# Layer 1 of a four-layer kernel: f and g projected by image row into four bands of 32 partitions, bias and "plus one" on ScalarE, one tanh per row group

## The reference, cut to what matters

```python
def _L1_conv_ref(x, Wf, bf, Wg, bg, Wh, bh):      # Wf, Wg: 256 x 32, Wh: 256 x 256
    f = jnp.einsum('bhwc,ck->bhwk', x, Wf) + bf
    g = jnp.einsum('bhwc,ck->bhwk', x, Wg) + bg
    h = jnp.einsum('bhwc,co->bhwo', x, Wh) + bh
    scores = jnp.einsum('bhik,bhjk->bhij', f, g)   # 64 x 64 for each image row
    attn = jax.nn.sigmoid(scores)
    out = jnp.einsum('bhij,bhjo->bhio', attn, h)
    return out
def _L2_conv_ref(...):                             # the end of it
    gate = jax.nn.sigmoid(feats).reshape(b, h, w, 1)
    return gate * x
x = x + _L1_conv_ref(_gn(x), ...)
```

## Time and profile before

| what | value |
|---|---|
| median of three runs | 5786.15 us (5784.26 to 5790.85) |
| profiled execution | 5781.0 us, its span 5779.1 us |
| PE busy | 5346.3 us, 93% of the span |
| DVE busy | 4160.8 us, 72% |
| ACT busy | 4086.9 us, 71% |
| POOL busy | 1926.3 us, 33% |
| mean granted TensorE clock | 0.952 of full |

### The profile page before, as it was taken

The page is one execution under the profiler, slowest core; times in us unless marked ns, Lnnn a source line. Parts: engine busy times, 40 slices in busy tenths (PEclk is TensorE's granted clock), DMA queues, the critical chain, the costliest instruction groups (busy, mean ns, idle before and its releaser), DMA issues.

```text
span 5779.1 us, 111762 instructions
## 1 busy us (share of the span) xinstructions
PE 5346.3 (93%) x43240; PEld 2801.0 (48%) x43240; DVE 4160.8 (72%) x8715; ACT 4086.9 (71%) x6385; POOL 1926.3 (33%) x1588
## 2 busy tenths in 40 slices
PE   7799999989999999999999999999999999999886
PEld 3435445363553645446364453645446354453624
DVE  8467777777777777677777777777677777777726
ACT  1467768677786867768677785777868678686794
POOL 2224243342423424233341423424233242433402
PEclk9799999999999999999999999999999999999996
DMA  2010201102011020101102011020101102011000
GB/s 80 8 38 12 65 25 47 39 5 72 17 60 30 14 64 12 64 26 34 50 7 69 21 59 30 12 64 14 61 28 31 50 10 67 22 52 36 3 30 30
DMA packets 163165, 211.10 MB, mean 37 GB/s; under 512 B 13136, under 2 KB 146000, under 8 KB 162640
## 3 DMA queue, kind: packets, MB, share of 16 engines
q1 hardware_dynamic: 138064, 136.82, 7.3%
q0 software_dynamic: 24576, 67.14, 4.0%
HBM read 136.80 MB, written 67.11 MB: 35 GB/s over the span
## 4 chain that ended last, share of the span: by engine, by line
PE 70%; ACT 13%; DVE 9%; issue 5%; POOL 2%; DMA 1%; ACTq 0%; DVEq 0%; POOLq 0%; SPq 0%
PE PS L1190 34%; PE PS L1365 15%; PE PS L1356 6%; PE PS L1460 2%; ACT n_x L505 2%; PE PS L1224 2%; PE PS L1248 2%; PE PS L1299 2%; ACT big L579 1%; DVE stats L843 1%; ACT work L543 1%; ACT work L542 1%; ACT soft L579 1%; ACT xin L505 1%; ACT attn L551 1%
## 5 line engine op out<-in xcount | busy, mean ns | idle before, releaser
L579 ACT ACTIVATE big<-PS 128x1024 f32<-128x1024 f32 x1376 | 1365.3, 1024 | 458.9 <-PE PS L1356 397.2
L579 ACT ACTIVATE soft<-PS 128x1024 f32<-128x1024 f32 x672 | 676.0, 1024 | 359.3 <-PE PS L1356 349.9
L400 POOL DMA_INDIRECT quant_H<-emb_t,idx x512 | 487.4, 952 | 981.8 <-DVE idx L867 790.0
L1190 PE MATMUL PS<-e_hi,n_hi 128*128 128x512 f16 x2048 | 781.7, 382 | 20.2 <-DVE m L861 10.7
L1190 PE MATMUL PS<-e_lo,n_hi 128*128 128x512 f16 x2048 | 778.3, 380 | 0.0
L1190 PE MATMUL PS<-e_hi,n_lo 128*128 128x512 f16 x2048 | 778.1, 380 | 0.0
L1365 PE MATMUL PS<-big,w 128*4 128x512 f32 x5504 | 759.8, 641 | 0.0
L843 DVE BATCH_NORM_STATS2 stats<-XT 128x6 f32<-128x512 f32 x1024 | 651.7, 683 | 12.4 <-POOL XT L416 2.5
L867 DVE FIND_INDEX8 idx<-m,work 128x8 uint32<-128x1024 f32 x512 | 622.2, 1219 | 0.0
L1356 PE MATMUL PS<-rhs,lhs 12*128 12x512 bf16 x4096 | 563.9, 398 | 59.6 <-ACT big L579 37.3
L861 DVE CUSTOM_DVE_ANT_0 work<-PS,e_bias,m 128x512 f32<-128x512 f32 x512 | 384.1, 750 | 213.1 <-PE PS L1190 207.1
(11 more groups left out here) (216 smaller groups left out, 11134.1 us busy)
## 6 DMA issues: line engine op xcount, KB each, us to landing
xin<-x SPq DMA_DIRECT2D x128, 512.0 KB, 3.8
out<-yout SPq DMA_DIRECT2D x128, 512.0 KB, 2.9
quant_H<-emb_t,idx POOLq DMA_INDIRECT x512, 2.7
XT<-emb SPq DMA_DIRECT2D x1, 1024.0 KB, 6.0
XT<-wh SPq DMA_DIRECT2D x1, 256.0 KB, 5.9
XT<-wqv SPq DMA_DIRECT2D x1, 256.0 KB, 6.2
XT<-wk SPq DMA_DIRECT2D x1, 128.0 KB, 6.1
w_sb<-w SPq DMA_DIRECT2D x1, 128.0 KB, 5.9
```

Source lines behind the costliest of these rows:

```text
L400: nc.gpsimd.indirect_dma_start(quant[:, g % 2, u, :], None, emb_t, bass.IndirectOffsetOnAxis(ap=idx[:, t % (2 * GT), 0:1], axis=0),).then_ ...
L579: nc.scalar.activation(E[h % 3][:, z * 1024:(z + 1) * 1024], bank(2 * z, 2), ACT.Exp).then_inc(exped.sem, 1)
L1190: ins = mm(dst, a, b, start=first and j == 0, stop=last and j == 2)
```

## The change

Four things change; the lists of steps are the same.

1. `l1_fg` on PE goes by image row. f and g of even rows (r = 0) and odd rows (r = 1) go to four bands of 32 partitions in bank 4: f of r = 0, f of r = 1, g of r = 0, g of r = 1. Each band takes six products of 32 rows by 256 columns, whose moving operand picks four runs of 64 pixels with a stride of 128. That is 24 matmuls for a group. The bias product goes away, with onesel, its memsets and the setup that splits the bias.
2. ACT moves f (64 x 256) and g (64 x 256) with one instruction each, and adds the bias in it from a column of 64 floats. FT and GTm lie on partitions 0 to 63, r = 1 on 32 to 63; `l1_scores` reads them there. The bias comes by four DMAs of 32 floats in place of one of 96 x 64.
3. The tanh is one instruction of 128 x 256 into a new place (tanhs, part of work); the two that add 1 read it there and write the diagonal blocks.
4. Of the gate, ACT adds 1 itself, behind its exponential, and DVE only takes the reciprocal.

```diff
-        FT = work[0:CK, 0:1024].rearrange("p (s w n) -> p s w n", s=2, w=2)
-        GTm = work[0:CK, 1024:2048].rearrange("p (s w n) -> p s w n", s=2, w=2)
+        FT = work[0:2 * CK, 0:512].rearrange("p (s n) -> p s n", s=2)
+        GTm = work[0:2 * CK, 512:1024].rearrange("p (s n) -> p s n", s=2)
+        tanhs = work[:, 1024:1536].rearrange("p (s n) -> p s n", s=2)
...
-                (bfg_f, bfg.partition_broadcast(96)),
                 (bo_f, b_out.partition_broadcast(P)),
+                *((fg_bias[(2 * j + w) * CK:(2 * j + w + 1) * CK, :], bfg[j * CK:(j + 1) * CK].unsqueeze(1))
+                  for j in range(2) for w in range(2)),
...
             def l1_fg(im, g):
                 act.wait_ge(*l1_scored.room(im, g, 2))
                 act.wait_ge(*l1_fged.after(im, g))
-                for w in range(2):
-                    r = 2 * CK * w
-                    nc.scalar.activation(FT[:, g % 2, w, :], PS[r:r + CK, 4, 0:2 * P], copy)
-                    last = nc.scalar.activation(GTm[:, g % 2, w, :], PS[r + CK:r + 2 * CK, 4, 0:2 * P], copy)
+                if im + g == 0:
+                    act.wait_ge(weights_in, 16 * NW)
+                for j, kept in enumerate((FT, GTm)):
+                    rr = slice(2 * CK * j, 2 * CK * (j + 1))
+                    last = nc.scalar.activation(kept[:, g % 2, :], PS[rr, 4, 0:2 * P], copy, bias=fg_bias[rr, 0:1])
                 last.then_inc(l1_fgkept.sem, 1)
...
-                for r in range(2):
-                    rr = slice(r * ROW, (r + 1) * ROW)
-                    last = nc.scalar.activation(attn[rr, g % 2, :, rr],
-                                                PS[rr, 4, 0:GT * ROW].rearrange("p (u i) -> p u i", u=GT), ACT.Tanh, scale=0.5)
-                last.then_inc(l1_tanhed.sem, 1)
+                nc.scalar.activation(tanhs[:, g % 2, :], PS[:, 4, 0:GT * ROW], ACT.Tanh, scale=0.5).then_inc(l1_tanhed.sem, 1)
                 act.wait_ge(*l1_tanhed.after(im, g))
                 for r in range(2):
                     rr = slice(r * ROW, (r + 1) * ROW)
-                    last = nc.scalar.activation(attn[rr, g % 2, :, rr], attn[rr, g % 2, :, rr], copy, bias=ones[rr, 0:1])
+                    last = nc.scalar.activation(attn[rr, g % 2, :, rr], tanhs[rr, g % 2, :].rearrange("p (u i) -> p u i", u=GT),
+                                                copy, bias=ones[rr, 0:1])
...
             def gate_exp(im):
                 act.wait_ge(*gate_arg.after(im))
                 nc.scalar.activation(gate[:, 1, :], gate[:, 0, :], ACT.Exp, scale=-1.0).then_inc(gate_exped.sem, 1)
+                act.wait_ge(*gate_exped.after(im))
+                nc.scalar.activation(gate[:, 1, :], gate[:, 1, :], copy, bias=ones[:, 0:1]).then_inc(gate_oned.sem, 1)
...
-                dve.wait_ge(*gate_exped.after(im))
-                link(v.tensor_scalar(gate[:, 1, :], gate[:, 1, :], 1.0, None, ALU.add))
+                dve.wait_ge(*gate_oned.after(im))
                 v.reciprocal(gate[:, 2, :], gate[:, 1, :]).then_inc(gate_made.sem, 1)
...
-                products = [(fg_bias, None)]
+                products = []
                 for k in range(KC):
                     products += [(fg_hi[:, k, :], n_hi[:, g % 2, k, :]), (fg_hi[:, k, :], n_lo[:, g % 2, k, :]),
                                  (fg_lo[:, k, :], n_hi[:, g % 2, k, :])]
                 for j, (weight, part) in enumerate(products):
-                    for w in range(2):
-                        moving = onesel[:, 0:2 * P] if part is None else part[:, w * 2 * P:(w + 1) * 2 * P]
-                        ins = mm(PS[64 * w:64 * w + 64, 4, 0:2 * P], weight[:, 0:2 * CK], moving,
-                                 start=j == 0, stop=j == len(products) - 1)
+                    for f in range(2):
+                        for r in range(2):
+                            rr = slice((2 * f + r) * CK, (2 * f + r + 1) * CK)
+                            ins = mm(PS[rr, 4, 0:GT * ROW], weight[:, f * CK:(f + 1) * CK],
+                                     part.rearrange("p (u r i) -> p r u i", u=GT, r=2)[:, r, :, :],
+                                     start=j == 0, stop=j == len(products) - 1, skip_group_check=True)
...
                 for u in range(GT):
                     for r in range(2):
-                        cols = slice(u % 2 * P + r * ROW, u % 2 * P + (r + 1) * ROW)
-                        ins = mm(PS[r * ROW:(r + 1) * ROW, 4, u * ROW:(u + 1) * ROW], GTm[:, g % 2, u // 2, cols],
-                                 FT[:, g % 2, u // 2, cols], start=True, stop=True)
+                        cc, cols = slice(r * CK, (r + 1) * CK), slice(u * ROW, (u + 1) * ROW)
+                        ins = mm(PS[r * ROW:(r + 1) * ROW, 4, cols], GTm[cc, g % 2, cols], FT[cc, g % 2, cols],
+                                 start=True, stop=True)
```

More of the change, by code:

```diff
@@ L110, in build @@
         ones = sb("ones", [P, P])
-        onesel = sb("onesel", [96, 2 * P], BF16)
         mhalf = sb("mhalf", [P, GT])
@@ L117, in build @@
         fg_lo = sb("fg_lo", [P, KC, 2 * CK], F16)
-        fg_bias = sb("fg_bias", [96, 2 * CK], BF16)
+        fg_bias = sb("fg_bias", [P, 1])
         h_hi = sb("h_hi", [P, KC, C], F16)
@@ L250, in build @@
         filled, exped, summed = step("filled", 2 * HALVES), step("exped", 2 * HALVES, 2), step("summed", HALVES, 3)
-        acc_kept, acc_turned, gate_arg, gate_exped, gate_made = (
-            step(n, 1) for n in ("acc_kept", "acc_turned", "gate_arg", "gate_exped", "gate_made"))
+        acc_kept, acc_turned, gate_arg, gate_exped, gate_oned, gate_made = (
+            step(n, 1) for n in ("acc_kept", "acc_turned", "gate_arg", "gate_exped", "gate_oned", "gate_made"))
         g_normed, g_spread = step("g_normed"), step("g_spread")
@@ L298, in build @@
         wfg_f = xt_w[:, 5376:5504].rearrange("p (k n) -> p k n", k=KC)
-        rows_r = xt_w[0:96, 5504:5568]
-        bfg_f = xt_w[0:96, 5568:5632]
         bo_f = xt_w[:, 5632:5888]
@@ L303, in build @@
         wmean = xt_w[:, 6144:6148]
-        NW = 12
+        NW = 15
         @block.sync
@@ L763, in link @@
                 dve_chain.link(dve, ins)
-            for t, val in ((ones, 1.0), (mhalf, -0.5), (attn, 0.0), (w2, 0.0), (ctxd, 0.0), (onesel, 0.0), (m8, BIG)):
+            for t, val in ((ones, 1.0), (mhalf, -0.5), (attn, 0.0), (w2, 0.0), (ctxd, 0.0), (m8, BIG)):
                 setup_link(v.memset(t[:], val))
             setup_link(v.memset(bank(4), 0.0))
-            for j in range(3):
-                setup_link(v.memset(onesel[32 * j:32 * j + 1, :], 1.0))
             for f in range(2):
@@ L798, in prepare @@
                 if part == 3:
-                    for j in range(3):
-                        rr = slice(32 * j, 32 * j + 32)
-                        setup_link(v.tensor_copy(fg_bias[rr, :], bfg_f[rr, :]))
-                        for q in range(j + 1, 3):
-                            tail = slice(32 * q, 32 * q + 32)
-                            setup_link(v.tensor_copy(rows_r[tail, :], fg_bias[rr, :]))
-                            setup_link(v.tensor_tensor(bfg_f[tail, :], bfg_f[tail, :], rows_r[tail, :], ALU.subtract))
                     setup_link(v.tensor_reduce(wmean[:, 0:1], wo_f, AX, ALU.add))
```

## The result

The changed kernel takes 5632.5 us (median of 4 runs, 5627.4 to 5634.2) where the kernel before takes 5785.2 beside it (4 runs, 5780.0 to 5790.9): 0.9734 of the time, 95% interval 0.9718 to 0.9751. The forecast was 5671 us, with a range from 5636. The direction held; the gain was 153 us where 115 were forecast, and the time fell 3.5 us under the range's lower end.

The account below looks back on a forecast made before the run. PE, 93% busy, bounds it, alternating with ACT in layer 1's stretches. Fifteen stretches x 7.3 = 110 us, with 3 from the first stretch and 2.5 setup, 115 less: 5666, plus 5 to the median, 5671 us; range 5636 to 5738.

Parts of the forecast that it names:

- Copies: ACT's copies of f and g: two at 0.468 us replace four of 0.375, 0.56 us less a group.
- Tanh: ACT's tanh in layer 1: one of 128 x 256 replaces two of 0.378 us, 0.38 us less a group.
- The gate's add on ScalarE: Gate's plus one, 2.151 us on DVE, takes 0.30 on ACT: chain 1.85 us shorter in fifteen images.
- The reciprocal at its own length: DVE's reciprocal behind the gate's add is not stalled by POOL; if it were, all 1.85 us would stay.
- Projections: PE's f and g products: seven pairs become six fours at 0.11 us each, 0.9 us less a stretch.
- Scores: Layer 1's eight fp32 score products on PE stay at 0.68 us a group.
- The idle: PE's idle in a layer 1 stretch: half of today's 8.1 us stays, 4.0 us, giving 59.9 us a stretch.
- The clock: Lower clock costs PE some 3.8 us in thirteen of fifteen layer 1 stretches; 2.6 come back, 2.3 us a stretch.
- lower end: Fastest bound: 2 us of PE idle a stretch, 9.3 us less each, 147 less in all, 5639 us.
- Rival 1: PE's idle in layer 1 stretches stays as DVE and PE wait for each other: 52 us less, 5734; chance 0.16.
- Rivals 2, 3 and 4: Fours two by two, about 5755 us (0.05); scores one by one, 5730 (0.07); fours one by one, 5890 (0.05).
- Rival 4's turning point: Change turns slower where a group's projections cost over 0.77 + 0.8 us, a four above 0.26 us.

Follow-up runs that it names:

- e5: Changed kernel with each copy of f and g cut in two (32 partitions each): 5735.4 us.
- e6: Changed kernel with the tanh cut in two instructions of 64 x 256: 5683.4 us.
- e7: Changed kernel with one spare product of all four bands in each group's projections: 5639.7 us.
- e2: Kernel before with only the gate's plus one moved to ScalarE: 5739.1 us.
- e3: Changed kernel with the gate's plus one back on DVE: 5692.4 us.
- e12: e3 with fifteen idle-filling products on PE ahead of its wait for the gate: 5675.2 us.
- e1: Kernel before with fifteen idle-filling products on PE ahead of the gate's wait and fifteen ahead of the third group's scores: 5737.5 us.
- e10: Changed kernel with five idle-filling products ahead of each of the first waits for an exponential in the distances: 5626.2 us.
- e9: Kernel before with the edits of e1 and e2 together: 5736.0 us.
- e11: Changed kernel with the lower 64 partitions of the tanh's plus one moved to DVE as a tensor-tensor add: 5785.1 us.
- e4: Changed kernel with attn as two 64-row halves, output products in two row groups, one plus-one instruction, DVE's sum in four instructions: 5761.0 us.

## Why the prediction fell short

Step by step, as the prediction put them:

- Copies, forecast 0.468 us: 0.465. Tanh 0.38: 0.383. The gate's add on ScalarE 0.30: 0.321. The reciprocal at its own length: 0.353. All right. On the chain the prediction took the copies of six groups and the tanh of five; e5 and e6 bear that out at 2.4 GHz (4.94 us for 5.6, 2.33 for 1.9). Scaled to what the change itself saved (0.56 of e5's 0.93, 0.38 of e6's 0.37), they give an estimate of 3.0 and 2.4 us a stretch; with 1.5 for the gate that is 6.9, where the stretch at 2.4 GHz fell by 5.83, so the parts overlap somewhat.
- Projections, 0.11 a four: measured so, and e7 prices one at 0.094. PE's busy time at 2.4 GHz fell by 1.21 us a stretch where 0.9 was counted, 5 us in fifteen. Scores unchanged at 0.68. The rule on row tiles and PSUM banks that the prediction named, from "TensorEngine Tiling (Array Packing)" in the Trainium skill, did not cost the 0.46 us a group: here the two row tiles write different partitions of one bank, and the trace disagrees with the rule for that case.
- The idle. Forecast 4.0 us a stretch, measured 3.79. "Half of today's idle" was a choice between the bounds of 2 and 8.1 and not worked out, so that it fell so near is in part luck. One term ahead of it was too large: it took the gate's 1.85 off the chain of the kernel before, where e2 shows it worth 0.8. Once ScalarE's 7.5 us are gone, which is the case that was forecast, it is worth 1.4 to 1.5 (e3, e12).
- **The clock, the step that failed.** "I count 2.6 of the 3.8 back in thirteen of fifteen: 2.3 us a stretch." The prediction gives no reason for the 1.2 that it holds back, and they came back too: PE's busy time lost 3.34 us a stretch through the clock, as much as 3.8 in thirteen of fifteen (3.3), and e1 had 3.4 by filling two idles. The idles that the change leaves (in the stretch shown) are at most 1.3 us long, and no lower clock followed in fourteen of fifteen stretches. Fifteen x (59.9 - 58.4) = 22 us of the miss are in the stretches, and 15 x 1.04 = 16 of them are this term.
- Nothing was counted outside the stretches, and 15 us came from there, spread over the gaps. The edits don't reach these instructions. What differs is the time at the lower clock in them, 304 us before and 239 after, above all at the start of the distances; e3's pair of gaps shows what such a piece costs when it grows. By time, 10 of the 15 us lie in four gaps (the fourth, seventh, twelfth and fourteenth), which before had 6.8 or 10.2 us at the lower level near their end and 3.4 after. That the gaps' 15 us are all of this kind is not shown: e10 has the least lower clock of all and only 2.3 us less there than the changed kernel. No run sets where these pieces fall.
- The first stretch gave 3.9 instead of 3, the setup 2.6 instead of 2.5.
- The range. Its lower end took 2 us of idle but the same 2.3 us of clock, although the rows had a price of 3.8 for it. With the full clock the lower end would have been 15 x 1.5 = 22 us deeper.

Rival 1 was wrong: DVE's sum does release the longest wait, but at about its old size. Rivals 2, 3 and 4 were denied by the times of the fours and the scores. Rival 4's turning point, 0.8 us more a group, is a little low: the 115 us of the forecast are 0.9 for each of 128 groups.

## What to carry to other kernels

Where a lower granted clock stands behind TensorE's idles, a shorter wait pays twice. Take the whole difference between stretches at the two levels as one end of the range, and look at the stretches behind the changed one too. Fill the idle with products of no use, once, to measure that part by itself, but not ahead of a wait that another edit shortens: the products then hold the engine up in its place (e9). Where a loop repeats, compare repetitions that ran at the same clock. The same shorter wait was worth 0.8 us in one kernel and 1.5 in the other, because the engine next in line had more or less room, so price an edit in the kernel that has the other edits.

## What was not expected of the hardware

- The same fill of the distances ran 13.7 us at 1.2 GHz in one image and 3.4 in the next (e3), with 3.8 us between the two gaps and no instruction changed between them.
- Fifteen products that filled one idle of 2 us took the lower level away in nine of fifteen stretches and left 3.4 us of it in six (e12).
- A DVE add of 0.42 us whose two inputs lie in SBUF took up to 2.15 beside POOL (e11).
- Two row groups side by side at fp32 with 64 columns gave no more than one with 128 (e4: 259.2 against 258.2 us); the weight loads, 189 ns for 64 rows and 192 for 128, did not get shorter with half the rows.
